# Chunked cross-attention on one core: met waits that set the matmul engine's instruction count per block to 640 and shift it by ninety

## The chip, the cores and the metric

The kernel runs on one core of a Trainium2 chip. The metric is the device time of one execution in microseconds (us). The matmul engine is TensorE; the profile shows it as PE (matmuls) and PEld (weight loads, which run beside matmuls). DVE is VectorE, ACT ScalarE, POOL GpSimd, and SP SyncE, which here issues every transfer.

## The reference

The input `x` and the context are 32 batches of 256 channels by 2048 tokens, all fp32. Queries, keys and values are all projected from the context; attention is within chunks of 64 tokens, 8 heads of 32 channels; then comes an output projection, a mask, the residual `x`, and a normalisation over each channel's 2048 tokens.

```
Wq, Wk, Wv = split(W_in, 3);  q = ctx.T @ Wq.T + bq;  k, v alike      # ctx: (32, 256, 2048)
scores = einsum('bnqhd,bnkhd->bnhqk', q, k) / sqrt(32) + where(mask > 0, 0, -1e9)
out = einsum('bnhqk,bnkhd->bnqhd', softmax(scores), v) @ W_out.T + b_out
out = out.transpose(0, 2, 1) * masks + x
result = (out - mean(out, axis=2)) * rsqrt(var(out, axis=2) + 1e-5)
```

## The kernel before

The program is one straight line of instructions on each engine, written out by Python loops and without branches. The tokens of a batch fall into four blocks of 512 (`BLOCKS`), each of two units of 256 tokens (`UNITS` is 8), each of four chunks. In step `u` of a batch the matmul engine (function `steps` under `@block.tensor`) runs, in this order: `scores` of unit `u + 1`; then for an even `u` `project_out` of two blocks back, for an odd one `project_k` of two blocks ahead; `probs_times_v` of unit `u - 2`; and for an even `u` `project_v`, for an odd one `project_q`.

Two steps, an even one and the odd one behind it, make one **block** of the engine's program, and this text counts a block from the first matmul of its even step's `scores`. In matmuls as the profile counts them, a block is: 64 of `scores` (L383), 12 of `project_out` (L365), 64 of `probs_times_v` (L416), 24 of `project_v` (L342), 64 of `scores`, 12 of `project_k` (L308), 64 of `probs_times_v`, 12 of `project_q` (L308). That is 316, and each has a weight load of its own, so 632 instructions. The fp32 matmuls of L383 and L416 become two passes each. An instruction can carry one wait; what more a matmul has to wait for stands in front of it as instructions of their own that only wait, up to two conditions in each. Of these a block has seven. So there are 639 instructions from one block to the next, and 81,844 of loads, matmuls and waits in the whole program of the engine.

The four blocks of a batch period are called A (steps 4 and 5), B (6 and 7), C (0 and 1) and D (2 and 3) here; the first block that has a `project_out` is an A. They are alike on the matmul engine. They differ on SP, whose `steps` reads:

```
if h == 1:
    if j >= 2:
        load_mask(j + 2)
    move_values(j + 1)
    if j >= -2:
        load_ctx(j + 6)
elif j >= 3:
    load_x(j - 1)
store(BLOCKS * (B - 1) + u - 6 if u >= 6 else BLOCKS * (B - 2) + u + 2 if u < 2 else -1)
move_probs(B, u)
```

`load_ctx` (L194), `load_x` (L211) and `store` (L230) move 512 KB each, `load_mask` (L203) 256 KB, `move_values` (L241) 256 KB in two transfers, and `move_probs` (L256) four times 64 KB. Stores stand in steps 6, 7, 0 and 1 alone. SP issues in this order, and each issue may wait for a semaphore. All transfers, and the fetches of instructions too, share the core's 16 DMA engines.

At the start the matmul engine waits for `pool_const` (two small fills by GpSimd), zeroes the score banks (`open_banks`, L394), and waits for the split weights and the split context of the first block before its first product (L308).

Of the kernel before, what the change touches and what calls it, by code (L numbers as in the profile page):

```python
# [25 lines left out]
TPU = UNIT // P  # L26
SLOTS = ROWS * CPU
EPS = 1e-5
SCALE = DH ** -0.5


# [10 lines left out]
def attention_kernel(nc, x, ctx_in, mask, w_in_t, b_in, w_out_t, b_out, out):  # L42
    stack = ExitStack()
    with stack:
# [6 lines left out]
        def sem(name):  # L51
            return stack.enter_context(nc.semaphore(name))
# [56 lines left out]
        pool_const = sem("pool_const")  # L109
# [45 lines left out]
        def count(B, per, n):  # L155
            return B * per + n
# [4 lines left out]
        def unit_there(B, u):  # L161
            return there(B, u, UNITS)
# [131 lines left out]
        def _(pe):  # L294
            def output_bias():
                pe.wait_ge(w_loaded, 32)
                pe.wait_ge(wo_loaded, 32)
                for f in range(HALVES):
                    for h in range(HALVES):
                        last = pe.matmul(o_bank[:, 1, f:f + 1], wo_raw[:, h, f * P:(f + 1) * P],  # L300
                                         b_cols[:, 4 + h:5 + h], start=(h == 0), stop=(h == 1))
                last.then_inc(pe_const, 1)
# [9 lines left out]
            def project_q(B, n, f):  # L312
                if not block_there(B, n):
                    return
                pe.wait_ge(k_f_done, count(B, 2 * BLOCKS, 2 * n + f + 1))
                project_qk(B, n, f, q_proj, 0)

            def project_k(B, n, f):
                if not block_there(B, n):
                    return  # L320
                if f == 0:
                    pe.wait_ge(ctx_hi_done, count(B, 2 * BLOCKS, 2 * (n + 1)))
                    pe.wait_ge(ctx_lo_done, count(B, 2 * BLOCKS, 2 * (n + 1)) - 1)
                    if BLOCKS * B + n == 0:
                        pe.wait_ge(ctx_lo_first, 1)
                if block_there(B, n - 1):
                    pe.wait_ge(v_f_done, count(B, 2 * BLOCKS, 2 * (n - 1) + f + 1))
                project_qk(B, n, f, k_proj, C)
# [18 lines left out]
            def project_out(B, m, f):  # L347
                if not block_there(B, m):
                    return
                if f == 0:  # L350
                    if BLOCKS * B + m == 0:
                        pe.wait_ge(dve_const, 5)
                    pe.wait_ge(o_hi_done, count(B, UNITS, UPB * (m + 1)))
                if block_there(B, m + 3):
                    pe.wait_ge(q_f_done, count(B, 2 * BLOCKS, 2 * (m + 3) + f + 1))
                elif block_there(B, m + 2):
                    pe.wait_ge(v_f_done, count(B, 2 * BLOCKS, 2 * (m + 2) + f + 1))
                else:
                    pe.wait_ge(y_done, count(B, 2 * BLOCKS, 2 * (m - 1) + f + 1))
                terms = [(wo_hi, o_hi), (wo_lo, o_hi), (wo_hi, o_lo)]  # L360
                for a, (w, o) in enumerate(terms):
                    if f == 0 and a == 2:
                        pe.wait_ge(o_lo_done, count(B, UNITS, UPB * (m + 1)))
                    for h in range(HALVES):
                        last = pe.matmul(proj_bank[:, f, :], w[:, h, f * P:(f + 1) * P], o[:, m % 2, :, h, :],  # L365
                                         start=(a == 0 and h == 0), stop=(a == 2 and h == 1))
                last.then_inc(out_proj, 1)

            def scores(B, u):
                if not unit_there(B, u):  # L370
                    return
                j, h = u // UPB, u % UPB
                if h == 0:
                    pe.wait_ge(q_f_done, count(B, 2 * BLOCKS, 2 * (j + 1)))
                    pe.wait_ge(k_f_done, count(B, 2 * BLOCKS, 2 * (j + 1)))

                pe.wait_ge(seeded, count(B, UNITS, u + 1))
                for c in range(CPU):
                    tokens = slice(h * UNIT + c * CHUNK, h * UNIT + (c + 1) * CHUNK)
                    for r in range(ROWS):  # L380
                        head = slice(r * DH, (r + 1) * DH)
                        for f in range(HALVES):
                            last = pe.matmul(score_bank[f * CHUNK:(f + 1) * CHUNK, r, c * CHUNK:(c + 1) * CHUNK],  # L383
                                             q_f[head, j % 2, f, tokens], k_f[head, j % 2, f, tokens], start=False,
                                             stop=True, skip_group_check=True)
                last.then_inc(rows_done, 1)

            def open_banks():


                for r in range(ROWS):
                    head = slice(r * DH, (r + 1) * DH)
                    for f in range(HALVES):
                        last = pe.matmul(score_bank[f * CHUNK:(f + 1) * CHUNK, r, 0:UNIT], zero_rows[head, 0:CHUNK],  # L394
                                         zero_rows[head, :], start=True, stop=True, skip_group_check=True)
                last.then_inc(opened, 1)

            def probs_times_v(B, u):
                if not unit_there(B, u):
                    return  # L400
                j, h = u // UPB, u % UPB
                n = BLOCKS * B + j
                pe.wait_ge(v_f_done, 2 * n + h + 1)
                pe.wait_ge(v_moved[n % V_RING], 32 * (n // V_RING + 1))

                if n == 0:
                    pe.wait_ge(dve_const, 5)
                wait(pe, o_lo_done, UPB * n + h)
                pe.wait_ge(moved[u % UNITS], 64 * (n // BLOCKS + 1))
                for c in range(CPU):  # L410
                    for r in range(ROWS):
                        for f in range(HALVES):
                            keys = slice(f * CHUNK, (f + 1) * CHUNK)
                            at = (f * P if c % 2 == f else 0) + r * DH
                            values = (v_f if c % 2 == f else v_x)[keys, n % V_RING, h, c // 2, at:at + DH]
                            last = pe.matmul(o_bank[r * DH:(r + 1) * DH, f, c * CHUNK:(c + 1) * CHUNK], values,  # L416
                                             prob_t[keys, u % 2, :, r * CPU + c, :],
                                             start=True, stop=True, skip_group_check=True)
                last.then_inc(pv_done, 1)

            pe.wait_ge(pool_const, 2)
            open_banks()
            pe.wait_ge(dve_const, 2)

            def steps(B):
                for u in range(UNITS):
                    j, h = u // UPB, u % UPB
                    scores(B, u + 1)
                    for f in range(HALVES):
                        if h == 0:  # L430
                            project_out(B, j - 2, f)
                        else:
                            project_k(B, j + 2, f)
                    probs_times_v(B, u - 2)
                    if B < 0 and u == 6:
                        output_bias()
                    for f in range(HALVES):
                        if h == 0:
                            project_v(B, j + 1, f)
                        else:  # L440
                            project_q(B, j + 2, f)

            batches(steps)

        @block.scalar
        def _(act):
# [22 lines left out]
            def exponentials(B, u):  # L469
# [3 lines left out]
                part = prob[:, u % 2, :, :, :].rearrange("p r c k -> p (r c k)")  # L473
                act.activation(part, part, ACT.Exp, scale=SCALE).then_inc(exp_done, 1)  # L474

# [161 lines left out]
        def _(dve):  # L637
# [74 lines left out]
            def mean_and_variance(B):  # L712
# [6 lines left out]
                dve.wait_ge(mean_done, count(B, 2, -1))  # L719
                dve.tensor_scalar(var_eps[:, :], mean_var[:, :, 1], EPS, None, ALU.add).then_inc(mean_done, 1)  # L720

# [65 lines left out]
```

## Time and profile before

| | us |
|---|---|
| median of 3 runs | 2021.92 |
| lowest and highest | 2021.39, 2031.84 |
| the profiled execution | 2024.09 |
| its span, first to last instruction | 2022.3 |

The rows of the trace are of the profiled execution; its span is 1.8 us shorter than its own time and 0.4 us above the median of the runs. In the rows, a group is: start in us, length in us, engine, line, operation, output and inputs, how many instructions; and in brackets the idle time ahead of it and what ended it. "issue" is time in which the engine waited for nothing that the profile shows.

### The profile page before, as it was taken

What the parts mean: (1) busy time and instruction counts of PE and PEld (TensorE: products, weight loads), DVE (VectorE), ACT (ScalarE), POOL (GpSimd) and SP (SyncE); (2) the same over time, 40 slices, a digit from 0 to 9 for tenths busy, and PEclk for the clock granted to TensorE, in tenths of its full rate; (3) what the DMA queues carried; (4) which work ended last, traced back from release to release, by engine and by line L of the source; (5) the groups of instructions that cost most, each with busy time, mean ns of one, the idle gap of its engine ahead of it and who ended that gap; (6) DMA issues with size and microseconds to landing.
All of it is one profiled execution on the core that took longest, in us unless ns stands there. A gap on an engine that the chain in (4) does not pass through costs nothing.

```text
span 2022.3 us, 91553 instructions
## 1 busy us (share of the span) xinstructions
PE 1967.5 (97%) x40472; PEld 1597.4 (79%) x40472; DVE 1764.8 (87%) x2217; ACT 1565.7 (77%) x2176; POOL 1489.3 (74%) x1059
## 2 busy tenths in 40 slices
PE   7999999999999999999999999999999999999995
PEld 6888888777778888888878888888878778788883
DVE  5888988888888898888989889898889888888886
ACT  5778778777778877878777787777878778877773
POOL 4677777867777777777777777777776777777774
PEclk9999999999999999999999999999999999999997
DMA  4455666556665566665556666566655566655654
GB/s 157 128 160 174 169 187 181 166 147 169 181 179 165 161 173 181 186 180 168 163 173 184 172 177 173 165 171 187 180 163 160 171 177 177 170 172 165 173 147 146
DMA packets 242890, 342.55 MB, mean 169 GB/s; under 512 B 28992, under 2 KB 94784, under 8 KB 242496
## 3 DMA queue, kind: packets, MB, share of 16 engines
q1 hardware_dynamic: 242496, 336.71, 57.8%
q8 instruction: 319, 5.23, 1.0%
q14 instruction: 75, 0.61, 0.1%
HBM read 168.82 MB, written 67.11 MB: 117 GB/s over the span
## 4 chain that ended last, share of the span: by engine, by line
PE 96%; issue 2%; DVE 1%; POOL 0%; DMA 0%; ACT 0%; SPq 0%; DVEq 0%; POOLq 0%; ACTq 0%
PE proj_bank L308 38%; PE proj_bank L342 19%; PE proj_bank L365 18%; PE score_bank L383 11%; PE o_bank L416 10%; DMA b_cols<-b_in 0%; POOL y L590 0%; DVE row_max L658 0%; DVE stats L709 0%; DVE y L700 0%; POOL prob L572 0%; DVE w_lo L641 0%; DVE y L736 0%; DVE o_lo L689 0%; DVE prob L662 0%
## 5 line engine op out<-in xcount | busy, mean ns | idle before, releaser
L572 POOL TENSOR_TENSOR prob<-prob,recip 128x1024 f32<-128x1024 f32 x256 | 487.4, 1904 | 498.6 <-DVE recip L673 498.6
L658 DVE TENSOR_REDUCE row_max<-score_bank 128x16 f32<-128x1024 f32 x256 | 313.5, 1225 | 185.5 <-PE score_bank L383 181.8
L474 ACT ACTIVATE prob<-prob 128x1024 f32<-128x1024 f32 x256 | 271.6, 1061 | 235.2 <-DVE prob L662 235.2
L308 PE MATMUL proj_bank<-ctx_hi,w_hi 128*128 128x512 f32 x1024 | 349.2, 422 | 12.6 <-DVE ctx_lo L644 9.2
L580 POOL TENSOR_TENSOR ctx_lo<-ctx_raw,ctx_hi 128x512 fp32r<-128x512 f32 x255 | 329.6, 1293 | 18.2 <-ACT ctx_hi L454 18.2
L590 POOL TENSOR_TENSOR y<-y,x_raw 128x512 f32<-128x512 f32 x256 | 325.9, 1294 | 7.6 <-DVE y L700 7.5
L308 PE MATMUL proj_bank<-ctx_lo,w_hi 128*128 128x512 f32 x1024 | 322.6, 396 | 0.3 <-issue 0.3
L308 PE MATMUL proj_bank<-ctx_hi,w_lo 128*128 128x512 f32 x1024 | 319.9, 393 | 1.3 <-issue 1.3
L662 DVE TENSOR_TENSOR prob<-score_bank,row_max 128x1024 f32<-128x1024 f32 x256 | 313.4, 1224 | 8.8
L681 DVE STREAM_TRANSPOSE squares<-prob 128x1024 f32<-128x1024 f32 x256 | 315.8, 1234 | 1.5 <-POOL prob L572 1.5
L669 DVE TENSOR_REDUCE sums<-prob 128x16 f32<-128x1024 f32 x256 | 304.9, 1191 | 1.2 <-ACT prob L474 1.1
L507 ACT ACTIVATE k_f<-proj_bank,b_cols 128x512 f32<-128x512 f32 x256 | 174.2, 681 | 136.5 <-PE proj_bank L308 136.5
L490 ACT ACTIVATE prob_t<-squares 128x1024 f32<-128x1024 f32 x256 | 270.3, 1056 | 1.6 <-DVE squares L681 1.6
L466 ACT ACTIVATE score_bank<-neg_rows 128x1024 f32<-128x1024 f32 x256 | 262.6, 1026 | 0.0
L416 PEld LDWEIGHTS o_bank<-prob_t,v_f 64*32 64x32 f32 x8192 | 180.0, 106 | 100.4 <-issue 100.1
L383 PEld LDWEIGHTS score_bank<-k_f,q_f 32*64 32x64 f32 x16384 | 199.7, 131 | 73.6 <-issue 51.9
L604 POOL TENSOR_SCALAR neg_rows<-mask_all 128x512 f32<-128x512 f32 x128 | 246.5, 1926 | 0.0
L383 PE MATMUL score_bank<-k_f,q_f 32*64 32x64 f32 x16384 | 235.6, 231 | 10.1 <-ACT score_bank L466 5.9
L308 PEld LDWEIGHTS proj_bank<-ctx_hi,w_lo 128*128 128x128 f32 x1024 | 193.4, 189 | 46.7 <-issue 1.4
L416 PE MATMUL o_bank<-prob_t,v_f 64*32 64x64 f32 x8192 | 222.1, 224 | 8.0 <-DVE o_lo L689 5.0
L308 PEld LDWEIGHTS proj_bank<-ctx_lo,w_hi 128*128 128x128 f32 x1024 | 193.0, 188 | 44.9 <-issue 1.5
L342 PE MATMUL proj_bank<-w_hi,ctx_hi 128*128 128x256 f32 x1024 | 219.5, 296 | 0.3 <-DVE y L700 0.2
(46 smaller groups left out, 3691.9 us busy)
## 6 DMA issues: line engine op xcount, KB each, us to landing
ctx_raw<-ctx SPq DMA_DIRECT2D x128, 512.0 KB, 5.8
x_raw<-x SPq DMA_DIRECT2D x128, 512.0 KB
prob_t<-squares SPq DMA_DIRECT2D x1024, 64.0 KB, 2.5
out<-y SPq DMA_DIRECT2D x128, 512.0 KB, 6.9
mask_all<-mask SPq DMA_DIRECT2D x128, 256.0 KB, 4.2
v_x<-v_f SPq DMA_DIRECT2D x256, 128.0 KB, 3.5
y<-w_in_t SPq DMA_DIRECT2D x1, 768.0 KB, 5.7
y<-w_out_t SPq DMA_DIRECT2D x1, 256.0 KB, 6.7
```

What stands on the lines that cost most here:

```text
L308: last = pe.matmul(proj_bank[:, f, :], w[:, h, col + f * P:col + (f + 1) * P], c[:, n % 2, h, :], start=(a == 0 and h == 0), stop=(a == 2 ...
L342: last = pe.matmul(proj_bank[:, f, t * C:(t + 1) * C], c[:, n % 2, h, tok:tok + P], w[:, h, 2 * C:3 * C], start=(a == 0 and h == 0), stop= ...
L365: last = pe.matmul(proj_bank[:, f, :], w[:, h, f * P:(f + 1) * P], o[:, m % 2, :, h, :], start=(a == 0 and h == 0), stop=(a == 2 and h == 1))
L383: last = pe.matmul(score_bank[f * CHUNK:(f + 1) * CHUNK, r, c * CHUNK:(c + 1) * CHUNK], q_f[head, j % 2, f, tokens], k_f[head, j % 2, f, t ...
L416: last = pe.matmul(o_bank[r * DH:(r + 1) * DH, f, c * CHUNK:(c + 1) * CHUNK], values, prob_t[keys, u % 2, :, r * CPU + c, :], start=True, ...
L572: pool.tensor_tensor(part, part, slots(recip[:, u % 2, :]), ALU.mult).then_inc(norm_done, 1)
L580: pool.tensor_tensor(ctx_lo[:, n % 2, :, tokens], ctx_raw[:, n % BLOCKS, :, tokens], ctx_hi[:, n % 2, :, tokens].bitcast(F32), ALU.subtrac ...
L590: pool.tensor_tensor(part, part, x_raw[:, m % 2, f, :], ALU.add).then_inc(added, 1)
L658: dve.tensor_reduce(row_max[:, :].rearrange("p (r c) -> p r c", c=CPU), rows, AX_X, ALU.max).then_inc(max_done, 1)
L662: dve.tensor_tensor(prob[:, u % 2, :, :, :], rows, slots(row_max[:, :]), ALU.subtract).then_inc(less_done, 1)
L669: dve.tensor_reduce(sums[:, :], prob[:, u % 2, :, :, :].rearrange("p r c k -> p (r c) k"), AX_X, ALU.add).then_inc(sums_done, 1)
L681: dve.transpose(squares[:, u % 2, :, :, :], prob[:, u % 2, :, :, :].rearrange("p r c (b j) -> p b (r c) j", j=SQ)).then_inc(turned, 1)
```

## The change

Two constants and a helper on the matmul engine. `pool_const` reaches 2 once, at the start, and never changes again, so every wait for it behind `open_banks` is met when it is reached. The helper asks for it again and again; two such waits go into one instruction.

```
+PIECE_WAITS = 1
+LEAD = 180
...
-            pe.wait_ge(pool_const, 2)
+            def met(waits):
+                for _ in range(waits):
+                    pe.wait_ge(pool_const, 2)
+
+            met(1 + LEAD)
             open_banks()
             pe.wait_ge(dve_const, 2)
 
             def steps(B):
                 for u in range(UNITS):
                     j, h = u // UPB, u % UPB
+                    if h == 0:
+                        met(PIECE_WAITS)
                     scores(B, u + 1)
```

Ninety instructions that only wait come in front of the first zeroing matmul. One more comes at the head of every block: the `scores` of an even step had one condition, which its first matmul carried, and now has two. No matmul, no transfer and no instruction of another engine is added, removed or moved. A block has 640 instructions now. All lines behind the two constants move down by five.

At the head of a block the matmul engine's program before has this row for the end of `project_q`, and these for `scores`, `project_out` and the start of `probs_times_v` (a row is a line, an operation, its tiles and how many; in brackets the semaphores waited for):

```order
177 L308 MATMUL proj_bank<-ctx_lo,w_hi 128x512 x2
178 L383 MATMUL score_bank<-k_f,q_f 64x64 [waits seeded]
179 L383 MATMUL score_bank<-k_f,q_f 64x64 x31
180 L365 MATMUL proj_bank<-o_hi,wo_hi 128x512 [waits q_f_done,o_hi_done,dve_const]
181 L365 MATMUL proj_bank<-o_hi,wo_hi 128x512
182 L365 MATMUL proj_bank<-o_hi,wo_lo 128x512 x2
```

And now:

```order
177 L313 MATMUL proj_bank<-ctx_lo,w_hi 128x512 x2
178 L388 MATMUL score_bank<-k_f,q_f 64x64 [waits seeded,pool_const]
179 L388 MATMUL score_bank<-k_f,q_f 64x64 x31
180 L370 MATMUL proj_bank<-o_hi,wo_hi 128x512 [waits q_f_done,o_hi_done,dve_const]
181 L370 MATMUL proj_bank<-o_hi,wo_hi 128x512
182 L370 MATMUL proj_bank<-o_hi,wo_lo 128x512 x2
```

The second condition is the instruction that is new; all that stands behind it is the same, one place later per block. At the start of the engine's program the rows are, now:

```order
0 L298 UNCONDITIONAL_BRANCH
1 L399 MATMUL score_bank<-zero_rows 64x256 [waits pool_const]
2 L399 MATMUL score_bank<-zero_rows 64x256 x7
3 L313 MATMUL proj_bank<-ctx_hi,w_hi 128x512 [waits ctx_hi_done,pool_const,ctx_lo_done,ctx_lo_first,dve_const]
4 L313 MATMUL proj_bank<-ctx_hi,w_hi 128x512
```

The ninety stand ahead of row 1 and have no row of their own, since they wait for the same semaphore that it named before.

## Rows read from the trace of the kernel before

**Rows 1.** The page: busy us, share of the span and instructions of each engine.

```profile
PE 1967.5 (97%) x40472; PEld 1597.4 (79%) x40472; DVE 1764.8 (87%) x2217; ACT 1565.7 (77%) x2176; POOL 1489.3 (74%) x1059
```

**Rows 2.** The page's DMA queues: queue, kind, packets, MB, share of 16 engines.

```profile
q8 instruction: 319, 5.23, 1.0%
```

**Rows 3.** Timeline of PE: heads of the first and last whole block.

```profile
55.64 0.91 PE L383 MATMUL score_bank<-k_f,q_f 32*64 32x64 f32 x64
...
1969.79 0.91 PE L383 MATMUL score_bank<-k_f,q_f 32*64 32x64 f32 x64
```

**Rows 4.** Timeline of PE: one block without idle time, and the next one's head.

```profile
997.25 0.92 PE L383 MATMUL score_bank<-k_f,q_f 32*64 32x64 f32 x64
...
1001.07 0.24 PE L416 MATMUL o_bank<-prob_t,v_f 64*32 64x64 f32 x1
...
1006.32 0.62 PE L308 MATMUL proj_bank<-ctx_hi,w_lo 128*128 128x512 f32 x2
...
1012.48 0.91 PE L383 MATMUL score_bank<-k_f,q_f 32*64 32x64 f32 x64
```

**Rows 5.** Timeline of PE: a C block with the longest stall, and the next head.

```profile
391.55 0.92 PE L383 MATMUL score_bank<-k_f,q_f 32*64 32x64 f32 x64
...
402.87 0.33 PE L383 MATMUL score_bank<-k_f,q_f 32*64 32x64 f32 x2 [2.77 <-issue]
...
411.26 0.91 PE L383 MATMUL score_bank<-k_f,q_f 32*64 32x64 f32 x64
```

**Rows 6.** Timeline of PE: a stall four blocks behind the one of rows 5.

```profile
467.96 0.70 PE L308 MATMUL proj_bank<-ctx_hi,w_hi 128*128 128x512 f32 x2 [1.54 <-issue]
```

**Rows 7.** Timeline of PE and SP: a C block, page start at place 212.

```profile
583.15 0.91 PE L383 MATMUL score_bank<-k_f,q_f 32*64 32x64 f32 x64
...
586.17 0.58 SPq L211 DMA_DIRECT2D x_raw<-x  x1
...
593.94 0.39 PE L308 MATMUL proj_bank<-ctx_hi,w_lo 128*128 128x512 f32 x1 [1.32 <-issue]
```

**Rows 8.** DMA queues: window 587.0 to 591.4, then 591.5 to 591.7.

```profile
q1 hardware_dynamic: 672, 1.23, 89.9%
...
q8 instruction: 1, 0.02, 32.2%
```

**Rows 9.** Windows: us, busy time of each engine, PEclk, DMA share, GB/s.

```profile
404.70:407.90 3.20, 3.20 (x51) 2.18 (x54) 3.20 (x4) 2.24 (x3) 0.00 (x0) 0.50 0.81 216
```

**Rows 10.** Timeline and DMA windows: an A block, fetch at 365.0 to 365.2.

```profile
361.07 0.91 PE L383 MATMUL score_bank<-k_f,q_f 32*64 32x64 f32 x64
...
364.08 0.58 SPq L211 DMA_DIRECT2D x_raw<-x  x1
...
q8 instruction: 1, 0.02, 41.2%
```

**Rows 11.** The same of a D block, fetch at 108.9 to 109.1.

```profile
101.34 0.91 PE L383 MATMUL score_bank<-k_f,q_f 32*64 32x64 f32 x64
...
104.34 1.20 SPq L211 DMA_DIRECT2D x_raw<-x  x1
...
q8 instruction: 1, 0.02, 30.2%
```

**Rows 12.** The same of a B block, fetch at 324.6 to 324.8.

```profile
315.34 0.91 PE L383 MATMUL score_bank<-k_f,q_f 32*64 32x64 f32 x64
...
319.19 0.58 SPq L211 DMA_DIRECT2D x_raw<-x  x1
...
q8 instruction: 1, 0.02, 29.1%
```

**Rows 13.** Timeline of PE: the start.

```profile
1.12 1.16 PE L394 MATMUL score_bank<-zero_rows 32*64 32x256 f32 x16 [1.12 <-POOL zero_rows L564]
11.43 1.19 PE L308 MATMUL proj_bank<-ctx_hi,w_hi 128*128 128x512 f32 x2 [9.16 <-DVE ctx_lo L644]
```

**Rows 14.** Waits of PEld: us in total, times, longest.

```profile
PEld o_bank L416 <- issue: 101.5, 258, 3.5
```

## The prediction

> **What bounds the kernel now.** The page first: the matmul engine is busy 97% of the span [rows 1], so the time is its work plus its stalls. The work per block is read off a block without idle time: from head to head 1012.48 - 997.25 = 15.23 us [rows 4]. From the first whole block's head to the last one's are 1969.79 - 55.64 = 1914.15 us for 124 blocks [rows 3]; 124 x 15.235 (the median block is between 15.23 and 15.24) is 1889.1. So **25.0 us** of this stretch are stalls, in a few blocks, and they are all that an edit without any work can give back or add to.
>
> The reader should see next where they stand. The longest is 2.77 us of idle ahead of the last matmuls of `scores`, released by "issue": no semaphore, no operand, no engine [rows 5]. Four blocks later the stall stands two matmuls further on, ahead of `project_k`'s first [rows 6]. A stall tied to data would stay with one matmul; this one moves by one load and one matmul in two blocks. The engine's instructions are fetched in packets: 5.23 MB in 319 packets, 16.4 KB each, and the program has 81,844 instructions, so 64 bytes each and 256 in a packet [rows 2]. Five pages of 256 are 1280, two blocks are 1278: a page starts two instructions later in every second block. Counted through the built program, the stalls of [rows 5 to 7] stand ahead of instructions 15,813, 18,374 and 23,494, and those divided by 256 leave 197 or 198. So they are **waits for the next page of instructions**, and over the 31 batches the page starts have swept 124 places each, half of all the places there are.
>
> **When a page comes too late.** A page's fetch goes out when the engine enters the page before it. In the C block of [rows 7] a page starts at place 212 of the block (places are instructions counted from the head), inside `probs_times_v`, which begins 3.82 us after the head [rows 4]; so the fetch is asked for at about 3.9. The packet starts only at 591.6, 8.45 after the head; until then the 16 DMA engines were 90% busy with the 512 KB of `load_x`, issued at 586.17, and of the store behind it [rows 7, 8]. The engine goes on at 593.94, 2.34 us after the packet's start. It needed the page at 9.30 after the head: place 468 is the fourth matmul of `project_k`, 0.23 behind the third, which starts at 1006.32 - 997.25 = 9.07 [rows 4]. With F as the packet's start after the head, the stall is F + 2.35 - 9.30 = **F - 6.95**; here 1.50, and the block shows 593.94 - 583.15 - 9.30 = 1.49.
>
> **The change part by part.**
>
> *One wait more per block.* It is reached after `project_q`, twelve matmuls of 0.23 us, when the queued ones are far from used up; the seven that a block has now stand the same way, and the block of [rows 4] has no idle at all. Cost nothing; without that cover it would be 128 x 0.2 = 26 us by the end bound below.
>
> *Ninety at the start.* They run between the release at 1.12 and `open_banks`, which took 1.16 us, and there is room until 11.43: 9.15 us [rows 13]. The trace shows no wait instruction by itself. A plain one is issued in under 0.01 us (128 of `probs_times_v` in 0.8 us), which makes 0.8 us, hidden; the stop before `probs_times_v`, with two of them, is 101.5 / 258 = 0.39 us, so at most 0.2 each, 18 us, of which 9 would show [rows 14]. I take 0.1, about the middle: 9 us, just over the room with `open_banks` behind it, **+1** (0 to +9).
>
> *The pages.* This is the term that decides. With 640 a block, two blocks are exactly five pages, and the drift ends. Ninety instructions of lead and the first blocks' additions put the page starts, counted in the program as built, at places 84, 340 and 596 of every A and C block and at 212 and 468 of every B and D block, for all 31 batches. Before, the pages that begin at 212 and 468 fell in A or C alone ([rows 7] is exactly that place), so none of the new places in its kind of block has been run, and each is worked out from its neighbours:
> - Starts at 84, 340, 468 and 596 have next pages that are needed 7.7 to 12 us after the head that they belong to, or later, with 7.2 to 7.5 us of work in the page; the packets start at most 3 to 4 us after they are asked for. No stall; for 340 in C, some tenths in a few batches, **+1** in all.
> - The page from 212 to 468 has 5.4 us of work only (71 instructions of `probs_times_v`, all of `project_v`, 128 of `scores`). Whether it is late depends on `load_x`. If the page is asked for before the load's packets queue up, it comes at once: a page start at about 3.3 and the load issued at 3.01 gave a packet at 365.0 to 365.2, 4.0 after the head [rows 10]. Where the load was issued over 0.3 us ahead of it, it waits until the load (and the store) is through.
> - **D**: the load is issued about 3.0 after the head, 0.9 ahead of the page start; the packet starts at 108.92 - 101.34 = 7.6 [rows 11]. Six such fetches in the trace begin at 7.3 to 8.8, four of them at 7.3 to 7.6. Stall 0.65 in each of 31 batches: **20 us** (bounds: F as in A, 6.9, gives nothing; 8.5 gives 48).
> - **B**: the load is issued anywhere from 2.95 to 4.4, and a store follows. In one of them it is at 3.85, the packet at 324.69 - 315.34 = 9.35 [rows 12]. A page start at 3.9 is behind the load where that is issued before about 3.65, which is so in 17 of 31 B blocks of the trace, and ahead of it in 14. When behind, F is 7.6 to 10.4 in the B and C blocks, mean 8.55: 1.6 us. 17 x 1.6 = **27 us** (bounds 0 and 31 x 2.4 = 74).
> - **The clock.** After the 3 us stall the clock is granted at 0.50 for 3.2 us [rows 9], and the block of [rows 5] takes 411.26 - 391.55 = 19.71: 4.48 over, 3.0 of stall and 1.5 of slower matmuls. A 2.0 us stall has done it once more, those of 1.8 and less never. I count three such in B: **+5**.
>
> The sum: 20 + 27 + 1 + 5 = 53 in place of 25, and 1 at the start: +29 on the profiled execution's 2024.1 (span 2022.3). Laid on the median of the runs, 2021.9 + 29 = **2051**.
>
> The Trainium skill, page "Runtime: NRT & Kernel Launch", section "Instruction fetch mechanics", says that the sequencer fetches the next 256-instruction page while it runs the present one, and that a crossing is "mostly hidden". The size agrees with [rows 2]. That it is hidden does not hold in [rows 5 to 7]; by it alone both kernels would have no stall here, and the sum would be +1.
>
> **Rivals.**
> *Pages early (faster).* If SP issues `load_x` in B after 3.9, or its packets take longer to queue than the 0.3 us that I read, the B pages all come at once; if also D drains as A does, by 6.95, nothing is late. Then 25 us go and at most 12 come: 1998 to 2011. For it: 14 of 31 B blocks are on that side already, and a fixed pattern repeats whatever happens, so it can be all or none. Against it: D's six fetches. It decides at F = 6.95.
> *Even.* B is on time and D as forecast, or both somewhat smaller: 20 to 35 us in place of 25, 2012 to 2032. The same time comes if a page is not what the stalls wait for, or its size is another so that the drift stays: then the change does not do what its numbers say, and it is 2022 to 2023. The packets of [rows 2] and the remainders of 197 speak against that. The rule of the skill's page named above would end here too.
> *Clock.* If every B page waits behind load and store as the one of [rows 12], each stall is 2.4 us and each costs the clock 1.5 more: 31 x 3.9 + 20 - 25 = +116, 2138; a half of that is 2090. For it: the block of [rows 5]. Against it: stalls of 2 us and over were two in some twenty.
>
> **How the numbers follow.** Forecast (2033 to 2085) 0.50, pages early 0.20, even 0.20, clock 0.10. The range from 2006 to 2090 leaves out most of the clock's case and the lower part of pages early. A measurement of this kernel can tell 0.5%, about 10 us, from no change: faster 0.20, same 0.20, slower 0.60.
>
> **What would show it.** Right: stalls by "issue" at one matmul alone, `project_k`'s fourth, in B and D blocks and in no A block; blocks A and C of 15.23 us throughout; the packet of the fetch starting at 7.3 to 7.6 in D. Wrong: stalls that still wander (the page is not 256), a first product later than about 12.5 (a wait costs more than 0.11), or B and D free of idle, which would be the load arriving behind the fetch.

## The result, and the profile after

The changed kernel takes 2055.4 us (median; 2054.6 to 2057.0), the kernel before, run beside it, 2023.7 (2021.4 to 2031.8): a ratio of **1.0144, 95% interval 1.0121 to 1.0168**, so it is slower by 1.4%. The forecast was 2051, with 0.60 on a slower kernel.

The page of the changed kernel, the lines that answer to [rows 1] and [rows 2], the chain by engine, and the one group of matmuls that waits more than before (busy us, mean ns | idle us ahead of it, and what ended it):

```profile
PE 1975.5 (96%) x40472; PEld 1596.9 (78%) x40472; DVE 1766.3 (86%) x2217; ACT 1567.7 (76%) x2176; POOL 1490.1 (73%) x1059
q8 instruction: 320, 5.24, 1.0%
PE 95%; issue 3%; DVE 1%; POOL 0%; ACT 0%; DVEq 0%; POOLq 0%; ACTq 0%
L313 PE MATMUL proj_bank<-ctx_hi,w_lo 128*128 128x512 f32 x1024 | 325.8, 393 | 30.7 <-issue 30.6
```

Waits of the matmul engine (us in total, times, longest), the three that end by "issue":

```profile
PE proj_bank L313 <- issue: 30.6, 32, 2.0
PE score_bank L399 <- issue: 10.8, 1, 10.8
PE o_bank L421 <- issue: 7.8, 6, 2.3
```

The engine does the same 40,472 matmuls. Most of the idle time that ends by "issue" behind the start has come together at one line, `project_k`'s matmuls by `w_lo`: 30.6 us in 32 stops. Heads of the first and the last whole block, and the start, in the timeline of the matmul engine (start, us, what; compare [rows 3] and [rows 13]):

```profile
10.83 1.16 PE L399 MATMUL score_bank<-zero_rows 32*64 32x256 f32 x16 [10.83 <-issue]
11.92 1.22 PE L313 MATMUL proj_bank<-ctx_hi,w_hi 128*128 128x512 f32 x2
...
55.29 0.91 PE L388 MATMUL score_bank<-k_f,q_f 32*64 32x64 f32 x64
...
1998.17 0.91 PE L388 MATMUL score_bank<-k_f,q_f 32*64 32x64 f32 x64
```

From head to head are 1942.9 us; less 124 x 15.235 = 1889.1 these are **53.8 us of stalls**, where [rows 3] gave 25.0. The account of the profiled execution (2054.6, against 2024.1): +28.8 of stalls, -0.35 up to the first head, +2.1 behind the last head (54.6 against 52.5), together +30.5. Split by kind of block (heads, counted as in [rows 3]), by what each block takes over 15.235: A 1.2, **B 37.0**, C 0.5, **D 15.0**; before, A 2.2, B 0.8, C 19.2, D 2.8.

The 2.1 us behind the last head are slower matmuls, not stalls: the same 649 matmuls take 2.4 us more of busy time, at a lower granted clock (windows from the last head to the end, before and after; columns as in [rows 9], the clock is the third number from the end):

```profile
1969.79:2022.30 52.51, 27.38 (x649) 21.25 (x648) 34.70 (x50) 19.70 (x26) 25.86 (x21) 0.77 0.46 142
...
1998.17:2052.80 54.63, 29.77 (x649) 23.06 (x648) 34.74 (x50) 19.70 (x26) 25.89 (x21) 0.71 0.43 136
```

The thirteen traces fall into two groups here: five (the changed kernel, `piece_only`, `lead204`, `lead216`, `lead692`) need 54.6 to 54.9 us behind the last head, eight need 51.8 to 52.9. What puts a kernel into one of them isn't shown.

A typical B block: timeline of the matmul engine and of SP, then the DMA queues of 511.5 to 516.0 (kind: packets, MB, share) and of 516.05 to 516.35:

```profile
507.77 0.91 PE L388 MATMUL score_bank<-k_f,q_f 32*64 32x64 f32 x64
...
510.79 0.58 SPq L216 DMA_DIRECT2D x_raw<-x  x1
511.47 0.44 SPq L235 DMA_DIRECT2D out<-y  x1
...
516.83 0.39 PE L313 MATMUL proj_bank<-ctx_hi,w_lo 128*128 128x512 f32 x1
518.62 0.40 PE L313 MATMUL proj_bank<-ctx_hi,w_lo 128*128 128x512 f32 x1 [1.40 <-issue]
```

```profile
q1 hardware_dynamic: 532, 1.01, 79.5%
...
q8 instruction: 1, 0.02, 21.8%
```

The page that is late is the one that begins at place 468. It is asked for when the engine enters the page before it, at place 212 in `probs_times_v`; the trace does not record that moment, but the matmul at place 212 starts 4.0 after the head, at 511.8. `load_x` and `store` were issued at 510.79 and 511.47, just ahead of it, the 16 DMA engines carry 1.01 MB in the 4.5 us that follow, and the packet starts at 516.10, 8.33 after the head. The engine goes on 2.5 us later, 1.55 behind its schedule. The place is always the same: of the 31 B blocks 28 stop ahead of place 469, the first matmul of that page, 33.2 us together; of the D blocks 10, 3.6 us.

A kind of stall that the prediction did not have, in a D block (timeline of SP and of the matmul engine, then the windows behind it, columns as in [rows 9]):

```profile
663.27 0.61 SPq L199 DMA_DIRECT2D ctx_raw<-ctx  x1
663.99 0.47 SPq L235 DMA_DIRECT2D out<-y  x1
...
665.85 0.91 PE L388 MATMUL score_bank<-k_f,q_f 32*64 32x64 f32 x64
...
672.43 0.21 PE L421 MATMUL o_bank<-prob_t,v_x 64*32 64x64 f32 x1 [2.30 <-issue]
```

```profile
672.40:675.60 3.20, 3.17 (x49) 3.07 (x49) 1.40 (x3) 1.52 (x2) 2.31 (x2) 0.61 0.13 44
675.60:678.80 3.20, 3.20 (x79) 2.95 (x79) 0.28 (x1) 2.66 (x4) 2.07 (x2) 0.86 0.07 17
```

Here it is the page that begins at D's place 212. It is asked for when the engine enters the page from C's place 596; the matmul at that place starts 12.0 us after C's head, at 662.6, which is 3.2 ahead of D's head. C's odd step issues a context load and a store, 512 KB each, at 663.27 and 663.99, and the packet starts at 670.05, 4.2 after D's head. Four D blocks stop so, 8.1 us. What picks out these four isn't shown: in the C block with its head at 398.79 SP's context load and store stand at the same times after the head (12.66 and 13.38, here 12.68 and 13.39), and there the packet starts 14.8 after C's head, where it is 19.5 here.

Two of the four are followed by the lower of the two levels of the clock, 1.2 in place of 2.4 GHz:

```profile
673.10:676.40 3.30, 3.30 (x16) 3.30 (x17) 0.80 (x2) 2.05 (x4) 3.11 (x3) 0.50 0.05 15
```

The 0.61 and 0.86 above are averages over windows in which it held for a part. This block takes 4.02 over its 15.235, 2.57 of which is the stall.

### The profile page after: what moved, and what is told of

Read it like the earlier page. It is cut to its first block, busy times and chain, and to the rows that moved or that the text cites. A ratio compares the mean times of both kernels' runs of the same rounds, so it can differ in the third digit from the quotient of the medians.

```text
span 2052.8 us, 91776 instructions
## 1 busy us (share of the span) xinstructions
PE 1975.5 (96%) x40472; PEld 1596.9 (78%) x40472; DVE 1766.3 (86%) x2217; ACT 1567.7 (76%) x2176; POOL 1490.1 (73%) x1059
## 4 chain that ended last, share of the span: by engine, by line
PE 95%; issue 3%; DVE 1%; POOL 0%; ACT 0%; DVEq 0%; POOLq 0%; ACTq 0%
PE proj_bank L313 38%; PE proj_bank L347 19%; PE proj_bank L370 19%; PE score_bank L388 10%; PE o_bank L421 10%; POOL y L601 0%; DVE row_max L669 0%; DVE prob L673 0%; POOL prob L583 0%; ACT score_bank L477 0%; DVE stats L720 0%; DVE y L747 0%; DVE o_lo L700 0%; DVE squares L692 0%; PE score_bank L399 0%
## 5 line engine op out<-in xcount | busy, mean ns | idle before, releaser
L313 PE MATMUL proj_bank<-ctx_hi,w_lo 128*128 128x512 f32 x1024 | 325.8, 393 | 30.7 <-issue 30.6
L421 PE MATMUL o_bank<-prob_t,v_x 64*32 64x64 f32 x8192 | 215.1, 225 | 7.9 <-issue 7.8
```

The source lines that it names most:

```text
L313: last = pe.matmul(proj_bank[:, f, :], w[:, h, col + f * P:col + (f + 1) * P], c[:, n % 2, h, :], start=(a == 0 and h == 0), stop=(a == 2 ...
```

## Experiments

Every kernel below is the changed one with the edit shown, except where it says otherwise. "Sum" is the stall time of the 124 whole blocks of the profiled execution, worked out as above from the first and the last head (of which those of the changed kernel stand above); places are counted in the program as built. Each sum is of one execution, each median of 2 to 12; the ratio is to the kernel before, run beside it.

| kernel | page starts in A, C / B, D | first head | sum (A, B, C, D) | median | ratio |
|---|---|---|---|---|---|
| changed | 84, 340, 596 / 212, 468 | 55.3 | 53.8 (1, 37, 1, 15) | 2055.4 | 1.0144 |
| piece_only | 174, 430 / 46, 302, 558 | 57.0 | 35.8 (1, 6, 1, 29) | 2038.3 | 1.0066 |
| lead_only | drift | 55.5 | 24.2 (3, 1, 10, 10) | 2021.2 | 0.9992 |
| lead204 | 72, 328, 584 / 200, 456 | 57.3 | 139.8 (2, 87, 3, 49) | 2137.1 | 1.0555 |
| lead216 | 66, 322, 578 / 194, 450 | 58.0 | 16.8 (1, 0, 7, 9) | 2016.0 | 0.9978 |
| lead228 | 60, 316, 572 / 188, 444 | 60.5 | 18.3 (1, 0, 14, 3) | 2021.3 | 0.9993 |
| lead692 | as changed | 83.4 | 46.1 (1, 33, 1, 11) | 2085.3 | 1.0312 |
| x_late | as changed | 55.2 | 44.7 (1, 5, 31, 8) | 2047.0 | 1.0134 |
| store_cd | as changed | 56.1 | 48.3 (1, 3, 2, 43) | 2050.5 | 1.0139 |
| lead216_even | as lead216 | 59.8 | 10.3 (0, 0, 1, 9) | 2013.2 | 0.9947 |
| lead228_even | as lead228 | 60.5 | 0.7 (1, 0, 0, 0) | 2014.8 | 0.9949 |
| before_even | drift | 57.5 | 28.3 | 2025.2 | 1.0004 |

**Each half alone.** `piece_only` has the wait per block and none at the start, `lead_only` the ninety instructions at the start and 639 a block.

```diff
-LEAD = 180
+LEAD = 0
```

> The changed kernel with LEAD = 0: 640 instructions per block as in it, but none of the ninety in front. Page starts stand still at places 174 and 430 of A and C blocks and 46, 302 and 558 of B and D blocks. Page theory (a page of 256 instructions that is fetched behind load_x comes too late where the page in front of it is short): no page is asked for between the load's issue and 9.3 us with a short page behind it, so nearly no stalls: 25 us of the kernel before go and some 3 come, 2002 us (1998 to 2008). Rival, that the extra wait in each block costs the time: 32 us over the kernel before as in the changed kernel, 2055. Rival, that it is the ninety at the start: 2023.

Measured 2038.3, ratio 1.0066 (1.0041 to 1.0091): slower, where a gain was expected (2002). The waits of the matmul engine (as above):

```profile
PE proj_bank L347 <- issue: 26.8, 27, 1.7
```

They stand in `project_v`, ahead of place 303 of 21 of the 31 D blocks (27.2 us), and of ten B blocks (4.5). SP's timeline around such a D block's head at 599.32:

```profile
597.30 0.61 SPq L199 DMA_DIRECT2D ctx_raw<-ctx  x1
598.35 0.38 SPq L235 DMA_DIRECT2D out<-y  x1
599.82 2.48 SPq L261 DMA_DIRECT2D prob_t<-squares  x4
```

The page that begins at 302 is asked for at the head, when the engine enters the one from 46, and behind the load and the store of C's odd step. Its packet starts 4.3 to 5.3 after the head in two thirds of the D blocks, the engine could go on at 6.7 to 7.6, and needs the page at 5.9. So the expectation had the mechanism and had left out that the transfers of an odd step can do what `load_x` does.

```diff
-PIECE_WAITS = 1
+PIECE_WAITS = 0
```

> The changed kernel with PIECE_WAITS = 0: ninety waits in front, 639 instructions per block, so that page starts drift again, from places 217 and 473 in B and D and 88, 344 and 600 in A and C. Page theory: B is late in the first four batches only (the page gets longer by 0.46 us with each batch), C in the last four, when its place comes to 200 to 212: 3 us and 11 us with a fall of the clock, and some 5 elsewhere; 19 in place of 25, 2017 us (2008 to 2030), with stalls that wander by two instructions in two blocks. Rival, that the ninety cost the time themselves: 2055.

Measured 2021.2, ratio 0.9992 (0.9978 to 1.0006), no change that can be told. The stalls wander again, over fourteen different matmuls, 24.2 us in all. **The loss is therefore in the fixed pattern, not in the start.** Of its 24.2, D has 10.0, nearly all of it where a page starts at a place from 24 to 64, behind C's odd step, as in `piece_only`.

**Other places of the fixed pattern.** The edit is one number, which moves all page starts together.

```diff
-LEAD = 180
+LEAD = 204
```

> The changed kernel with LEAD = 204: twelve wait instructions more in front, page starts of B and D at place 200 and 456. Page theory: the page is still asked for behind load_x (place 200 is reached when the array is at probs_times_v's first matmuls, 3.8 us), but needed at 8.3 in place of 9.3 us, so each stall is 1.0 longer: B about 2.1, D about 1.2, and every second B stall takes the clock down for 1.5 more: 31 x 3.3 + 24 = 126 in place of 54, 2125 us (2095 to 2150). Rival, that the changed kernel's loss has nothing to do with the place: 2055 + 1.

Measured 2137.1, ratio 1.0555 (1.0516 to 1.0594), inside the range that was expected. Twelve instructions move the time by 82 us. All 31 B blocks stop ahead of place 456 (56.8 us without the slower clock), 26 of D (24.6). Its waits:

```profile
PE score_bank L388 <- issue: 67.0, 53, 2.5
```

The line is another, the last matmuls of `scores`. The page is needed at about 8.5 after the head in place of 9.30 (402.87 - 2.77 - 391.55 = 8.55 for the last two of them in [rows 5]), but asked for hardly sooner, since twelve instructions of `probs_times_v` are under 0.1 us: 1.8 us a stall in B in place of 1.2. The granted clock of the whole execution is 0.973, against 0.990 for the changed kernel.

`lead228` and `lead216` go further the same way, until the fetch gets ahead of `load_x`. The page starts at 188 and 194 still lie in `probs_times_v`, whose matmul there starts 4.0 after the head. But the packets of B's pages start 2.7 to 4.0 after it in `lead228` and 3.3 to 4.1 in `lead216`, most of them before that matmul, so the engine takes its instructions in ahead of running them. The two edits:

```diff
-LEAD = 180
+LEAD = 228
```

> The changed kernel with LEAD = 228: twenty-four wait instructions more in front, page starts of B and D at place 188 and 444. Page theory: place 188 is entered while project_out runs, at about 2.4 us, ahead of load_x (issued at 2.9 or later), so the page comes at once in B and D: no stall there, 2 us elsewhere, and 3 us for 114 waits of 0.106 us at the start, which pass the room of 9.2 us there: 2003 us (1999 to 2012). Rival, that a later place is simply worse, in line with twelve more: over 2125.

```diff
-LEAD = 180
+LEAD = 216
```

> The changed kernel with LEAD = 216: page starts of B and D at 194 and 450, of A and C at 66, 322 and 578. With LEAD = 228 the only stalls left were in C, ahead of place 317 (14 us in 31 C blocks: the page from 60 to 316 waits behind the store of C's predecessor and is needed at 5.9). Six places less make that page 0.7 longer, so that some 3 us of stall stay there; in B and D place 194 is entered at about 3.0, with load_x issued at 2.9 or later, so the page still comes first, and those stalls stay away as at 188. Page theory: 4 us of stalls in place of 25 and 2 at the start, 2005 us (2000 to 2012), the fastest of all. Rival, that 194 is behind the load as 200 is: 2100 and over. Rival, that a later start gives a little less each time: 2021.

Both did in B what was expected: its stalls fall from 37.0 to 0.1 and 0.0. The time did not follow so far: 2021.3, ratio 0.9993 (0.9975 to 1.0011), where 2003 was expected, and 2016.0, ratio 0.9978 (0.9957 to 1.0000), where 2005 was; neither differs clearly from the kernel before. `lead228` has 14.1 us in C, 16 blocks ahead of place 317, and its first head comes 5.2 us later than the changed kernel's; `lead216` has 6.9 in C and 9.0 in D, and its first head 2.7 later. The added waits are 2.6 and 2.0 of these, at the 0.109 us found below; the rest of `lead228`'s isn't explained. The place of `lead228`'s stalls in the C block with its head at 519.77, SP and the matmul engine:

```profile
517.59 0.61 SPq L199 DMA_DIRECT2D ctx_raw<-ctx  x1
518.30 0.48 SPq L235 DMA_DIRECT2D out<-y  x1
...
528.00 0.39 PE L347 MATMUL proj_bank<-w_hi,ctx_lo 128*128 128x256 f32 x2 [1.43 <-issue]
```

Again the odd step ahead (B's), with a context load and a store; the page that begins at 316 is asked for behind them, when the engine enters the one from 60.

**The price of a wait.** 256 instructions more at the start leave every page start at its place.

```diff
-LEAD = 180
+LEAD = 692
```

> The changed kernel with LEAD = 692: 256 wait instructions more in front, exactly one page, so that every page start keeps its place. Page theory with 256 to a page: the same stalls in the same blocks, 53 us, and the first product later by 256 x 0.107 = 27.5: 2055 + 27.5 = 2083 us (2078 to 2088). Rival, a page of another size: stalls of another sum and at other matmuls. A wait that costs nothing once the first are met: 2055.

Measured 2085.3, ratio 1.0312 (1.0245 to 1.0378), from two executions that are 20 us apart (2075.2 and 2095.4); so the price is read off the trace. The start, as above for the changed kernel:

```profile
38.68 1.16 PE L399 MATMUL score_bank<-zero_rows 32*64 32x256 f32 x16 [38.68 <-issue]
39.77 1.22 PE L313 MATMUL proj_bank<-ctx_hi,w_hi 128*128 128x512 f32 x2
```

From 11.92 to 39.77 are 27.85 us for 256 instructions, 0.109 each; the first head moves by 28.1. The ninety are thus 9.8 us, and with the wait for the first product, at 11.43 before, nearly all of it is hidden. The stalls keep their places (25 B blocks and 10 D blocks ahead of 469) and are 46.1 in place of 53.8: the same pattern differs by 8 us between these two programs.

**Whose transfer it is.** `x_late` issues `load_x` in the odd step behind `load_ctx`; `store_cd` moves the stores from B and C to C and D.

```diff
-                    elif j >= 3:
-                        load_x(j - 1)
+                        if j >= 3:
+                            load_x(j - 1)
```

> The changed kernel with load_x moved on SP from the even steps to the odd ones, behind load_ctx; the matmul engine's program and its page starts are as in the changed kernel. If load_x is what the page at place 212 waits for, D's stalls go (15 us to 0) and B's shrink to what its store alone gives (37 us to some 5), while the odd steps carry 512 KB more and the page after place 596 comes later, which may cost 10: 2018 us (2005 to 2030). Rival, that pages are late whatever is issued around them, by a fetch time of their own: 2055.

B's stalls went as expected, from 37.0 to 4.6, none left ahead of 469; D's from 15.0 to 7.8, where 0 was expected: D has neither load nor store in its even step here, and the packet still starts 6.3 after its head in the middle block (6.9 in the changed kernel), so `load_x` is not all that it waits for. What was issued in the odd step before is left, and it wasn't tested apart. The packet in B starts 5.7 to 6.7 after the head in 28 of 31 blocks; in the changed kernel it is 5.2 to 9.7, mean 8.0. The total, 2047.0, ratio 1.0134 (1.0085 to 1.0184), missed: C has 31.3. The C block with its head at 768.04 (SP, then the matmul engine), and the DMA queues of 768.6 to 774:

```profile
766.42 0.61 SPq L199 DMA_DIRECT2D ctx_raw<-ctx  x1
767.08 0.55 SPq L216 DMA_DIRECT2D x_raw<-x  x1
767.72 0.41 SPq L235 DMA_DIRECT2D out<-y  x1
...
778.22 1.11 PE L388 MATMUL score_bank<-k_f,q_f 32*64 32x64 f32 x60 [2.19 <-issue]
```

```profile
q1 hardware_dynamic: 706, 1.29, 84.2%
```

Three transfers of 512 KB stand in a row. The page that begins at 340 is asked for when the engine enters the one from 84, within 1.0 us of the head (in the changed kernel its packet starts at 1.05 at the earliest), and in 14 of 31 C blocks the packet starts 6.2 to 7.6 after the head. The transfer was moved, and the queue with it.

```diff
-store(BLOCKS * (B - 1) + u - 6 if u >= 6 else BLOCKS * (B - 2) + u + 2 if u < 2 else -1)
+store(BLOCKS * (B - 2) + u if u < 4 else -1)
```

> The changed kernel with the four stores of a batch moved by two steps, from B and C to C and D; the matmul engine's program as in the changed kernel. If the store is what makes B's stalls longer than D's, the two change places: B some 15 us of stall in 31 blocks and D some 37, and the time stays, 2055 us (2045 to 2065). Rival, that B's stalls are of its place in the batch or of its own longer work: 37 and 15 as before.

Measured 2050.5, ratio 1.0139 (1.0104 to 1.0174), from two executions, and the kinds have changed places: B 2.5, D 43.4, 26 of its blocks ahead of 469. So **load and store together** make this page late: the load alone (B here) leaves 2.5 us in 31 blocks, the store alone (B in `x_late`) 4.6.

**Stores in even steps.** What `lead216` and `lead228` still lose was read as pages behind an odd step's store. The four stores of a batch go to the four even steps here; `lead216_even` and `lead228_even` are `lead216` and `lead228` with this edit, `before_even` is the kernel before with it alone.

```diff
-store(BLOCKS * (B - 1) + u - 6 if u >= 6 else BLOCKS * (B - 2) + u + 2 if u < 2 else -1)
+store(BLOCKS * (B - 1) if u == 6 else BLOCKS * (B - 2) + u // 2 + 1 if u in (0, 2, 4) else -1)
```

> The changed kernel with LEAD = 216 in place of 180 (page starts at 66, 322, 578 in A and C, at 194 and 450 in B and D), and the four stores of a batch, which go out in B's and C's even and odd steps, one each in the even steps alone (B, C, D, A). Theory (the stalls left with LEAD = 216, 16.8 us, are pages whose packet waits behind a store in an odd step, 6.9 in C and 9.0 in D): no odd step has a store, so both go; B had load and store in its even step already and no stall with these places, so A and D with the same load and store have none either. Stalls 2 to 5 us in all, first head as before at 58.0, so 2016 - 13 = 2003 (1998 to 2008). Rival (the packets waited behind other transfers of the odd steps, context loads, masks and moved probabilities, and the store was only there too): stalls of 12 to 17 us, 2012 to 2017.

> The same stores with LEAD = 228 (places 60, 316, 572 and 188, 444). Theory: C's 14.1 us of stalls ahead of place 317 are the page from 60 on behind the store of B's odd step, and go with it; D's 2.7 stay or go. Stalls 1 to 4 us in all, the first head at 60.5 as with LEAD = 228: 2021 - 15 = 2006 (2001 to 2011), some 3 slower than lead216_even for its later start. Rival (other transfers of the odd step): 14 us of stalls stay in C, 2018 to 2022.

> The kernel before, its page starts drifting by two each second block, with the four stores one each in the even steps. Theory: its stalls are pages behind load_x and the store of C's even step while a page starts near place 212, and that pair is still there, now in A and D too (B had it). Stalls 20 to 40 us in all in place of 25.0, so 2018 to 2038; the gain of lead216_even therefore needs the places and the stores together. Rival (the stores in odd steps are what costs, whatever the places): stalls under 12 us, 2003 to 2010.

`lead228_even` has a profiled execution of 2004.4 us (span 2002.5) with a sum of 0.7: C's 14.1 are gone. The windows from 60 to 1950 us (us, busy us of PE, PEld, DVE, ACT and POOL, granted clock, DMA share, GB/s):

```profile
60.00:1950.00 1890.00, 1889.80 (x39186) 1536.48 (x39185) 1698.66 (x2135) 1511.01 (x2105) 1439.00 (x1017) 1.00 0.61 173
```

The matmul engine is idle for 0.2 us in 1890. Its median, 2014.8, ratio 0.9949 (0.9928 to 0.9970), is 10 us above that execution (2004.4 to 2023.9 over nine), and above the 2001 to 2011 that was expected. The trace shows the fastest of the nine; the other eight have a mean granted clock of 0.989 to 0.992, this one 0.993, and where they lose 5 to 19 us stays open.

`lead216_even` has 2013.2, ratio 0.9947 (0.9926 to 0.9969). The expectation was 2003, and 2013 is inside its rival's range (2012 to 2017), by which the store in the odd step was only there too. The trace says both: C's 6.9 are gone (0.8), with the store. D's 9.0 are 9.4 now, in two blocks. In each of them the packet asked for at the end of the C block is late (17.4 after C's head in the first) with no store in that odd step, so the engine comes late to D's page start at 194, behind `load_x` and `store` now, and the next page is late as well: 3.06 and 2.25 of stall ahead of 451, and the lower clock behind. So a store in the odd step is not needed for that delay, and what causes it stays open.

`before_even` has 2025.2, ratio 1.0004 (0.9987 to 1.0020), sum 28.3, as expected: the stores alone bring nothing. **Places and stores together beat both kernels**, by 0.5% over the one before and 2% over the changed one. What the stores add to the places is clear from `lead228` to `lead228_even`; from `lead216` to `lead216_even` the intervals of the ratio still overlap.

## Why the prediction was right

- *The page starts decide, the wait itself costs nothing.* Right: C and A blocks have 0.5 and 1.2 us over 15.235 in 31 batches, wait included; and `lead_only`, which leaves the fixed pattern out, is even. The Trainium skill, page "Runtime: NRT & Kernel Launch", section "Instruction fetch mechanics", calls a crossing "mostly hidden"; by that rule twelve or eighteen instructions more at the start could not change 2055 into 2137 and 2016. The measurement decides.
- *B, 27 + 5.* It measured 37.0, 33.2 of it at the forecast matmul, and two errors offset each other. The number was low: 28 blocks, not 17, since SP issues `load_x` at 3.12 or earlier after the head in 27 of the 31 (in 9 of 31 before). That is the step that took the spread of the kernel before for that of the changed one; a pattern that repeats also repeats SP's moment. The size was high: 1.2 each in place of 1.6, the packet starting at 8.0 on average in place of 8.55. The clock fell behind one B block's stall, not three: 4.28 over, of which 2.18 and 0.64 are stalls and 1.5 the clock, the price that was assumed. That stalls of 1.8 us and less never lower the clock held in the trace of before only: in `lead_only` one of 1.7 did.
- *D, 20.* Measured 15.0, and for another reason in more than half. At the forecast place 3.6 us in 10 blocks, F being 4.8 to 8.2 with its median at 6.93, the bound itself: in the first half of the run it goes by turns, about 6.4 in one batch and 7.5 in the next. The six fetches that gave 7.6 were those of other places and the term was mis-sized. The other 8 us (11 with the clock) are the page from C's place 596. The sentence that failed is that starts at 84, 340, 468 and 596 "start at most 3 to 4 us after they are asked for": this one usually takes 2.8 from the matmul at place 596 (14.8 against 12.0 after C's head), and took 6.2 to 7.4 in four batches.
- *C, 1* was 0.5. *Start, +1*: the first product came 0.49 later and the first head 0.35 sooner. The price per instruction, taken as 0.1 between 0.01 and 0.2, is 0.109.
- *The sum*, 53 against 53.8, is thus better than its terms, and that is luck: B was 5 too low, D 5 too high. The mechanism was right, and B, the larger part, stands where it was forecast. The 2.1 us behind the last head were in no term; they are slower matmuls at a granted clock of 0.71 in place of 0.77.
- *The rivals.* "Pages early" is what `lead216` and `lead228` make of B; it needed the page start 18 or more instructions sooner. "Even" is `lead_only`. "Clock" is near `lead204`: all 31 B blocks late, clock 0.973, 2137 where the rival said 2138 for 31 stalls of 2.4.
- *What would show it.* One matmul alone: nearly (4 D and 3 B blocks stop ahead of place 213 too). A and C at 15.23: yes. Packet at 7.3 to 7.6 in D: no, in three of 31.

What is shown: the stalls follow the page starts (seven kernels that differ in the number of instructions), and their kind of block follows the transfers issued ahead (`x_late`, `store_cd`, the two with even stores). What is read from single traces only: that the packet waits in the DMA engines behind those transfers. Only the packet's start is in the trace; when it was asked for, and what it stood behind, is inferred. For the page asked for at C's last page start it isn't shown at all why four packets are late and others, behind the same issues, are not.

## What to carry to other kernels

When the bottleneck engine stops by "issue" at a matmul that has all its operands, count its instructions: if the stops stand at a fixed remainder, they are page starts, and what helped here was to keep the large transfers out of the moment at which a page is asked for, or the page start out of the moment of the transfers. A body of 640 instructions fixes that moment for the whole run, for better or worse: over five positions of the same body the time went from 2016 to 2137. So fix it only together with the order of the DMAs, and try some positions; left to drift, the stalls were 24 to 28 us in three kernels.

## What the runs showed of the hardware

- A wait that is already met costs the matmul engine 0.109 us when only waits are queued (256 of them: 27.85 us), some ten times a queued matmul of `probs_times_v`.
- A 16.4 KB packet of instructions can start over 5 us behind the matmul at whose place the page before it begins (B blocks of the changed kernel: 9.7 against 4.0 after the head, 8.0 on average), with 1.0 to 1.3 MB of other transfers going through the 16 DMA engines at 80 to 84%. The engine goes on some 2.3 us behind the packet's start (2.2 to 2.5 in 33 stops of the changed kernel).
- Long stalls were mostly, not always, followed by a lower granted clock. Over all traces, between the first and the last head, this was so within 2 us for 22 of 27 stops with 2.0 us of idle or more, and for 23 of 43 with 1.5 to 2.0; `lead228` has one of 2.07 without it. In the first such B block of the changed kernel (windows behind its stall of 2.02, columns as above) it is

```profile
143.70:146.90 3.20, 3.20 (x9) 2.41 (x8) 2.23 (x4) 1.63 (x2) 1.76 (x2) 0.55 0.62 164
146.90:150.10 3.20, 3.20 (x74) 2.31 (x73) 1.86 (x3) 2.43 (x4) 1.84 (x1) 0.92 0.84 226
```

at the 1.2 GHz level for most of the first window, then back: 1.5 us lost on top of the stall. In `lead204`, where such stalls are frequent, its stops ahead of 456 and 201 are 93 us of the 139.8, and most of the rest is this: the lower level was granted 25 times there.
